# A graph layer and a mixture of experts in one kernel: the first round of messages joins the early part

## The reference

```
def _layernorm(x): return (x - mean) / sqrt(var + 1e-5)

# x 625 x 512; src, dst, edge_type: 10625 edges; 8 relations, two directions
H_all = einsum('rod,nd->rno', W_rel, ln(x)) + b_rel       # 16 products, 625 x 512 each
agg   = segment_sum(H_all[rel, dst], src) + segment_sum(H_all[rel + 8, src], dst)
x     = x + relu(ln(x) @ W_self.T + b_self + agg)

logits = ln(x) @ router_w.T                                # 16 experts, top 2, softmax of the two
x = x + sum over the two experts of share * ((silu(ln(x) @ gate) * (ln(x) @ up)) @ down)
```

## Time and profile before

| what | value |
|---|---|
| median of three runs | 791.1 us (788.78 to 797.87) |
| the profiled execution | 788.58 us, its span 786.7 us |
| TensorE busy | 722.4 us (92%), 3293 instructions |
| VectorE busy | 631.8 us (80%), 1273 instructions |
| ScalarE busy | 446.9 us (57%), 626 instructions |
| GpSimd busy | 259.8 us (33%), 263 instructions |
| mean granted TensorE clock | 0.957 of full speed |
| HBM | 176.46 MB read, 27.80 MB written |

### The profile page before, as it was taken

How to read it: one execution, slowest core, us unless ns; L and a number is a source line. 1 busy time by engine, 2 the same in 40 slices (tenths; PEclk the granted TensorE clock), 3 DMA queues, 4 the chain that set the end, 5 groups by cost and what they waited for, 6 DMA issues and landing times. The chain is left out here.

```text
span 786.7 us, 11209 instructions
## 1 busy us (share of the span) xinstructions
PE 722.4 (92%) x3293; PEld 568.4 (72%) x3293; DVE 631.8 (80%) x1273; ACT 446.9 (57%) x626; POOL 259.8 (33%) x263
## 2 busy tenths in 40 slices
PE   3699999999999999999788578999999999999994
PEld 3467777777677777878456557888888888888883
DVE  6769859888698866666679689989999899999890
ACT  2222235554355556555543446778888888887771
POOL 2000027661477577777772000111111111111101
PEclk9599999999999999999789597999999999999998
DMA  6534458884688788888862479988989999999932
GB/s 190 180 88 149 133 152 267 265 264 158 221 288 273 260 248 280 294 289 275 272 188 81 171 272 406 365 291 300 349 291 357 376 380 364 378 380 375 385 129 27
DMA packets 52077, 204.77 MB, mean 260 GB/s; under 512 B 9422, under 2 KB 9422, under 8 KB 37444
## 3 DMA queue, kind: packets, MB, share of 16 engines
q1 hardware_dynamic: 33108, 145.69, 50.1%
q0 software_dynamic: 18928, 58.60, 25.9%
HBM read 176.46 MB, written 27.80 MB: 260 GB/s over the span
## 5 line engine op out<-in xcount | busy, mean ns | idle before, releaser
L544 POOL DMA_INDIRECT rows_sb<-h_dram,row_of x190 | 211.4, 1113 | 200.5 <-DMA h_dram<-h_sb 134.7
L671 ACT COPY h_sb<-p_h 125x512 f32<-125x512 f32 x80 | 46.9, 586 | 179.6 <-PE p_h L725 179.6
L613 DVE TENSOR_TENSOR rows_lo<-rows_sb,rows_hi 128x512 fp32r<-128x512 f32 x190 | 130.2, 685 | 14.9 <-ACT rows_hi L677 14.8
L723 PE MATMUL p_h<-wt_hi_sb,xt_hi 128*125 128x512 f32 x320 | 127.0, 397 | 0.6 <-DVE wt_lo_sb L565 0.6
L724 PE MATMUL p_h<-wt_lo_sb,xt_hi 128*125 128x512 f32 x320 | 126.9, 397 | 0.0
L725 PE MATMUL p_h<-wt_hi_sb,xt_lo 128*125 128x512 f32 x320 | 126.7, 396 | 0.0
L677 ACT CAST rows_hi<-rows_sb 128x512 fp32r<-128x512 f32 x190 | 106.5, 620 | 15.3 <-DMA rows_sb<-h_dram,row_of 15.0
L565 DVE TENSOR_TENSOR wt_lo_sb<-w_nat,wt_hi_sb 128x512 fp32r<-128x512 f32 x64 | 44.0, 692 | 68.6 <-ACT wt_hi_sb L665 68.5
L742 PE MATMUL p_sum<-rows_hi,seg_hot 128*125 128x512 f32 x190 | 82.1, 432 | 8.2 <-DVE rows_lo L613 7.0
L972 POOL DMA_INDIRECT tokens<-token_dram,rows_of_tokens x16 | 15.7, 981 | 211.0 <-ACT rows_of_tokens L1183 164.3
L1005 DVE TENSOR_TENSOR g_lo_sb<-stage_gate,g_hi_sb 128x2048 fp32r<-128x2048 f32 x34 | 76.4, 2285 | 1.4 <-DVE later_tiles L1112 0.7
(11 more groups left out here) (236 smaller groups left out, 1376.4 us busy)
## 6 DMA issues: line engine op xcount, KB each, us to landing
stage_up<-in_L_ffn_up_w SPq DMA_DIRECT2D x32, 1024.0 KB, 6.6
stage_gate<-in_L_ffn_gate_w SPq DMA_DIRECT2D x30, 1024.0 KB, 7.7
stage_down<-in_L_ffn_down_w SPq DMA_DIRECT2D x30, 1024.0 KB, 7.0
h_dram<-h_sb SPq DMA_DIRECT2D x80, 224.0 KB
w_nat<-in_L_gnn_W_rel SPq DMA_DIRECT2D x17, 1024.0 KB, 8.0
rows_sb<-h_dram,row_of POOLq DMA_INDIRECT x190, 4.7
h_dram<-h_sb SPq DMA_DIRECT2D x80, 26.0 KB
stage_gate<-in_L_ffn_down_w SPq DMA_DIRECT2D x2, 1024.0 KB, 7.4
```

The source lines that it names most:

```text
L544: nc.gpsimd.indirect_dma_start(rows_sb[:, b % ROWS], None, h_dram[0:1 + made(n) * TP], bass.IndirectOffsetOnAxis(ap=row_of[:, b:b + 1].bit ...
L613: v.tensor_tensor(rows_lo[:, b % PARTS], rows_sb[:, b % ROWS], rows_hi[:, b % PARTS].bitcast(F32), ALU.subtract).then_inc(part_lo, 1)
L671: s.copy(h_sb[:, i % OUTS], p_h[0:TP, i % 2]).then_inc(h_taken, 1)
L723: m.matmul(o, xt_hi[:, dc, at], wt_hi_sb[:, j % 2, dc], start=False, stop=False)
```

## The change

The early part and the first round of messages become one block. The functions on_sync, on_gpsimd, on_vector, on_scalar and on_tensor hold both and take a flag `later`; a loop `nc.Fori(1, rounds)` with `later` set follows behind a barrier, for rounds 2 and up, and runs no time with these inputs. What was a buffer of one piece is now allocated for both. The sums of all rounds stay in `p_sum`, so `carry` and `first` and their loads go; b_self becomes a seventeenth row of the biases and comes in with one more matmul per tile. `x2` is the buffer of x. The list work of VectorE is grouped: `list_columns` writes the five columns of a chunk. LISTS, START and PACE have other values.

```
-LISTS = ((1, 5.5), (18, 2.5))
-LAG, START, PACE = 3, 17, 3.0
-LOW, BIASES = 32, 2 * R
+LISTS = ((5, 6), (26, 3))
+LAG, START, PACE = 3, 26, 3.1
+LOW, BIASES = 32, 2 * R + 1

 # SyncE
 for row in (0, LOW):
-    sp.dma_start(bias_f[row:row + BIASES], b_rel).then_inc(bias_loaded, 16)
-w_load(sp, 0, first_w_loaded)
-for t in range(T):
-    sp.dma_start(carry[:, t], b_self ... .to_broadcast([TP, D])).then_inc(carry_loaded, 16)
+    sp.dma_start(bias_f[row:row + 2 * R], b_rel).then_inc(bias_loaded, 16)
+    sp.dma_start(bias_f[row + 2 * R:row + BIASES], b_self ...).then_inc(bias_loaded, 16)
+w_load(0)
+w_load(1)
...
 for j in range(2 * R):
     if j:
         sp.wait_ge(w_low, KC * j)
-    w_load(sp, j + 1, w_loaded[(j + 1) % 2])
+        w_load(j + 1)
+    if j == 2:
+        for i in range(2):
+            sp.dma_start(stage_gate[:, 2 * i:2 * i + 2], gate_w[0][i]).then_inc(loaded["g"][i], 16)
     for t in range(T):
         store(T * j + t)
-sp.wait_ge(w_low, KC * WEIGHTS)
-w_load(sp, 0, next_w_loaded)
-sp.wait_ge(next_w_loaded, 16)

 # VectorE
+buckets()
+dve.wait_ge(bias_hi, 1)
+v.tensor_tensor(bias_parts[LOW:LOW + BIASES], ...).then_inc(bias_ready, 1)
 dve.wait_ge(x_loaded, 32)
 normal(0)
 normal(1)
...
 for t in range(2, T):
     normal(t)
     scales(t)
     low_columns(t - 2)
+    if t == 2:
+        for dc in range(KC):
+            w_rest(0, dc)
...
+v.tensor_copy(crow[:], p_counts)
 ranks(0)
 low_columns(T - 2)
 low_columns(T - 1)
 blocks_and_told()
 ranks(1)
 ranks(2)
...
+for dc in range(KC):
+    w_rest(1, dc)
 places()
 for i in range(PRODUCTS):
     j, t = i // T, i % T
-    if t:
+    if j and t:
         w_rest(j + 1, t - 1)
     for d in range(2):
-        for c in range(columns(d, i), columns(d, i + 1)):
-            column(d, c)
+        for n in chunks(d, i):
+            list_columns(d, n)
         if columns(d, i - 1) < EC and columns(d, i) == EC:
             read_list(d)
+            if d == 0:
+                round_count()
     for b in range(due(i), due(i + 1)):
         message(b)

+def list_columns(d, n):
+    nth, wide = (EC // HOT) * d + n, IN_DIR[d]
+    if nth >= HOT_SETS:
+        dve.wait_ge(list_taken, nth - HOT_SETS + 1)
+    for k in range(HOT):
+        c = n * HOT + k
+        v.tensor_scalar(lane_hot[:, nth % HOT_SETS, k], slot_iota[:], lane[:, d, c:c + 1], None, ALU.is_equal)
...
+    i.then_inc(list_hot, 1)

-then(v.tensor_tensor(carry[:, t], p_sum[0:TP, t], carry[:, t], ALU.add))
-then(v.scalar_tensor_tensor(x2[:, t], carry[:, t], 0.0, x_sb[:, t], ALU.max, ALU.add))
+then(v.scalar_tensor_tensor(x2[:, t], p_sum[0:TP, t], 0.0, x_sb[:, t], ALU.max, ALU.add))

 # ScalarE: s.copy(bias_parts[:], bias_f[:]) now stands first
     if t >= 2:
         turned_high(t - 2)
+    if t == 2:
+        for dc in range(KC):
+            w_main(0, dc)
 scaled(T - 1)
 turned_high(T - 2)
 turned_high(T - 1)
+for dc in range(KC):
+    w_main(1, dc)
 for i in range(PRODUCTS):
     take(i)
...

 # TensorE
 turn_x(0)
 ranks(0)
+turn_x(1)
+turn_x(2)
+pe.wait_ge(bias_ready, 1)
 for i in range(PRODUCTS):
     product(i)                  # for j == 0 it also waits for xt_ready
+    if i < 2:
+        turn_x(3 + i)
+    if 1 <= i < 3:
+        ranks(i)
     for d in range(2):
         for n in chunks(d, i - 1):
             list_chunk(d, n)
     for b in range(due(i - 1), due(i)):
         message(b)
...
 def self_product(t):
+    bias(p_sum[0:TP, t], 2 * R, False)
```

More of the change, by code:

```diff
@@ L182, in build @@
             n_rounds = sb("n_rounds", [1, 1], I32, g)
[L184 to L237, removed]
-                        sp.dma_start(bias_f[row:row + BIASES], b_rel).then_inc(bias_loaded, 16)
-                    w_load(sp, 0, first_w_loaded)
-                    for t in range(T):
[L241 to L247, removed]
-                    for i in range(2):
-                        sp.dma_start(stage_gate[:, 2 * i:2 * i + 2], gate_w[0][i]).then_inc(loaded["g"][i], 16)
-                    sp.wait_ge(spare_cleared, 48)
-                    sp.wait_ge(small_loaded, 16)
-                    sp.wait_ge(carry_loaded, 16 * T)
-                    sp.wait_ge(first_w_loaded, 16)
-                @block.gpsimd
-                def _(pool):
-                    q = nc.gpsimd
@@ new lines, in due, with columns, chunks, token_columns @@
+            def due(i):
+                return taken[max(i, 0)]
+            def columns(d, i):
+                begin, each = LISTS[d]
+                return max(0, min(EC, int(each * (i - begin))))
+            def chunks(d, i):
+                return range(columns(d, i) // HOT, columns(d, i + 1) // HOT)
+            def token_columns(a, t):
+                return a[:, :, t * TP:(t + 1) * TP]
+            def turned(t):
+                return p_sum[:, 3 + t % 2, 0:KC * TP].rearrange("p (c n) -> p c n", c=KC)
@@ new lines, in on_scalar @@
+                    for i in range(PRODUCTS):
+                        j, t = i // T, i % T
+                        take(i)
+                        if j and t:
+                            if t == 1:
+                                act.wait_ge(w_low, KC * j)
+                            w_main(j + 1, t - 1)
+                        for b in range(due(i), due(i + 1)):
+                            message(b)
+                    for b in range(due(PRODUCTS), last_span):
+                        message(b)
@@ new lines, in on_tensor @@
+                    for b in range(due(PRODUCTS - 1), last_span):
+                        message(b)
+                    pe.wait_ge(small_loaded, 16)
+                for t in range(T):
+                    if not later:
+                        self_product(t)
+                    for k in range(last_in_tile):
+                        message(last_span + t * last_in_tile + k)
+                    if t:
+                        turn(t - 1)
+                    if t > 1:
+                        token_logits(t - 2)
```

812 lines of the change are left out of this document (426 added, 386 removed).

## The result

The changed kernel takes 1231.3 us, median of four runs (1229.2 to 1234.4), where the kernel before took 791.8 us on the same chip: a ratio of 1.554, 95% interval 1.544 to 1.564. The forecast was 805, the range 786 to 817. It was wrong by more than 400 us, and the sign alone was right. Ratios here leave out executions that lie more than 1.5% above the fastest of their kernel, medians in us do not, and the traces of the kernel with the condition, of the one with the hint and of the one with a lag of four are of such slower executions.

What follows compares the result with a forecast made beforehand. The prediction took VectorE's gated wait for ScalarE's high weight part, with list columns and messages behind it, to bound the kernel. Terms -12.0 + 5.2 + 25.3 - 2.4 - 0.7 + 1.5 = +16.9, taken as +15, gave 805 us, range 786 to 817.

Steps and rivals of the forecast that it cites:

- a jump across the unused loop body: Behind the message stage: the loop body for later rounds is jumped over, 0.6 us, between 0 and 4.
- -12.0 + 5.2: Start of the products: product 0 starts 12.0 us sooner (8 to 14); turns and ranks moved among products cost 5.2.
- Product 0's copy: Sign at the start of the products: the copy of product 0 would stand near 28 us.
- the moved work: Turns and ranks among first products cost 5.2 us, 1.2 of it stall; take(0) stands behind turned_high(4) and weight splits.
- The lists: Beside the products: writing list columns in chunks of five costs 25.3 us, rounded 25, bounds 5 and 32.
- Direction 0: First list, steps 5 to 19, no messages: TensorE waits for grouped chunks, cost 9.7 us.
- Direction 1: Second list, beside messages, steps 27 to 54, 17 chunks: grouped chunks come late, cost 15.6 us.
- The pattern: Sign where messages and list run together: copies of products 6.6 us apart behind a chunk.
- where messages begin and resume: Direction 1, steps 26, 42 and 43: about 5 us more lost, within the list term.
- rival 3: Chunk steps: TensorE's clock falls, four to six falls at 2.5 us a product, 815 to 820 us; chance 0.12.
- 2.4 and 0.7: End of the message stage: gains of 2.4 us without the carry and 0.7 without the reload of weight 0.
- Rivals 1 and 2: List stalls: 1, lists stay covered, 783 us, chance 0.18; 2, they grow by some 14, about 795 us, 0.12.

Runs made afterwards that it cites:

- the kernel with the condition: Changed kernel, its loop for later rounds entered only where the count of rounds is above 1; ratio 1.027 to the kernel before.
- the one with the hint: Changed kernel with single columns, earlier weight loads, direction 1's lists two steps sooner, later rounds under a compare with branch hint; 798.6 us, ratio 0.982.
- the one with a lag of four: The kernel with the hint, messages due four steps behind their product, not three, and 3.2 a step instead of 3.1; ratio 0.999.
- the one pair: Changed kernel without the later round, columns grouped in chunks of five against written one by one; ratios 1.024 and 0.994 to the kernel before.
- product 79 in the other: Pair of the kernel before with its loop from 1 and the kernel before with columns grouped in chunks; ratios 0.998 and 1.026.
- loop from 1: Kernel before, its loop over rounds counting from 1 instead of 0 to the same limit; ratio 0.998.
- grouped: Kernel before with one edit, the lists' columns written in whole chunks of five; ratio 1.026.
- rows apart: Changed kernel with its empty round, whose gathers read 128 rows that lie apart instead of row 0 128 times; 1217.3 us, ratio 1.493.
- again: Changed kernel unaltered, run once more on chip 1; 1252.3 us, ratio 1.544 to the kernel before.
- no round: Changed kernel with the loop for later rounds and its barrier taken out; 833.9 us, ratio 1.024 to the kernel before.

## Why the prediction was wrong

**The step that failed** is one clause of the end: "a jump across the unused loop body, which no row prices: 0.6, between 0 and 4". There was no jump. The body ran, 421.7 us: a loop from 1 to 1 makes one pass. I took the loop for one that tests first, and the trace of before could not correct me: one pass with a count of 1 is what either kind of loop shows. That the loop makes a pass all the same should have been a rival; no chance was kept for it. Its price stood in the rows: the drain holds 19 gathers in 25.0 us, 1.32 us each, so 250 us for 190, and 170 columns at 0.48 and 0.60 us are 92 more: some 340 us. And when the jump is made, it costs about 4.1 us, just above my upper bound of 4. The Trainium skill, Advanced Engine Details and Errata, Control Flow Timing, gives 0.05 to 0.11 us for a branch. This jump over a long body does not agree: 4.1 us.

**Without that step** the sum was +15 to +17, of which 1.5 were for barrier, load and jump. The kernel without the loop has none of these three and a ratio of 1.024, +19 us on 789 (13 to 24 by the interval); the one with the condition has all and 1.027, +22. So the rest of the sum was somewhat low, and part of its agreement is luck, as the terms show:

*The early part.* Timelines of the changed kernel's start:

```profile
13.18 0.68 DVE L522 TENSOR_TENSOR bias_parts<-bias_f,bias_parts 17x512 fp32r<-17x512 f32 x1 [2.14 <-ACT bias_parts L618]
```
```profile
25.36 0.63 PE L696 MATMUL p_h<-wt_hi_sb,xt_hi 128*125 128x512 f32 x1
...
29.34 0.59 PE L665 MATMUL p_sum<-ident,xn_whole 125*128 125x125 f32 x4
...
36.60 0.50 PE L683 MATMUL p_h<-bias_parts,select 128*125 128x512 f32 x1 [1.29 <-ACT h_sb L597]
```

Product 0's first real matmul starts at 25.36 against 35.57: 10.2 us sooner, not 12.0. The bias waited 2.14 us for its high part, and that for the load of b_self until 12.53, so the first statistics start at 13.89, 3.3 us later than the earlier trace rows, where I had 1.3. The moved turn took 0.35 us at the high clock (29.34 to 29.69; I had 0.5), and product 2 stands 1.29 us for ScalarE's copy, where I had 1.2. At the copy of product 2 the lead is 6.3 us; -12.0 + 5.2 had said 6.8. That is close partly by luck: the gain is 1.8 us smaller, and the cost up to there is 3.9. Product 0's copy, which I had wanted near 28 us, starts at 35.97, since it stands behind turned_high(4) and the weight splits on ScalarE; my own paragraph on the moved work said so, and the sign contradicted it.

*The lists.* Direction 0: 62.1 us against 50.1 before, from product 5 to 19 by the table, +12.0, forecast +9.7. (My parts, six of 1.0 to 1.1, two of 1.9 and one of 2.0, add up to 11.8 to 12.4 and not to the 11.4 that I wrote.) Direction 1: 197.3 against 173.0, +24.3, forecast +15.6. The pattern came as worked out: 6.67 us between copies where a chunk stands behind a message step, 4.40 where none does:

```profile
203.11 0.58 ACT L597 COPY h_sb<-p_h 125x512 f32<-125x512 f32 x1 [1.75 <-PE p_h L698]
209.78 0.59 ACT L597 COPY h_sb<-p_h 125x512 f32<-125x512 f32 x1 [3.93 <-PE p_h L698]
214.18 0.58 ACT L597 COPY h_sb<-p_h 125x512 f32<-125x512 f32 x1 [1.74 <-PE p_h L698]
```

Isolated, the grouping costs 21.9 us in the one pair (6.7 and 15.2 in the two directions) and 25.1 at product 79 in the other; I had 25.3. What I missed in direction 1 is a transfer:

```profile
139.76 0.62 ACT L591 CAST wt_hi_sb<-w_nat 128x512 fp32r<-128x512 f32 x1 [4.34 <-DMA w_nat<-in_L_gnn_W_rel]
```

The first ten gathers now go out beside a weight's load, and the two copies behind it are 7.0 and 7.3 us apart. I had about 5 us for where messages begin and resume, from VectorE's work alone; the weight was in no term. Where messages resume, the copies of products 43 and 44 stand 9.55 us apart: TensorE waits 1.86 us for the chunk and then makes its product at the lower clock (granted 0.56 from 232.6 to 236.5). The +24.3 holds for the first chip. On chip 2 the same stretch takes 196.5 us without the round and 183.4 in the kernel before with its loop from 1, +13.1, since there the kernel before loses time itself: its copies 43 and 45 come 9.95 and 8.27 us behind the one before. From product 22 to 79 it is 283.1 us against 259.7, +23.4, where I had 275 and +16.

*The clock, rival 3.* It fell, at 58.5 to 62 us and three times more up to product 57 (near 97, 141 and 233 us): 0.95 and 0.97 over the two list stretches where before it was 1.00. Rival 3, with a chance of 0.12, thus came true in large part, beside the forecast. At half speed for a tenth of 62 us and 6% of 197 that is an estimate of 3 + 6 us, part of the two excesses above. On chip 2 the kernel before, with its loop from 1, has 0.97 over its direction 1 too. The stall before the fall at 58.5 was 2.05 us, for the chunk of product 8's step.

*The end.* From the copy of product 79 to the logits 59.8 us against 61.7: gain 1.9, where 2.4 and 0.7 stood. That pair does not settle it: on the other chips this part takes 63.3 and 65.4 us in variants of the kernel before (loop from 1, grouped), and 66.4 to 72.1 in the changed kernel (rows apart, again, no round). So the gain is not shown beyond the first chip; the spread is larger than the term.

The range of 786 to 817 would have held a kernel with the loop tested first: 1.027 x 791.8 = 813.5. Rivals 1 and 2 are out: the grouping alone costs over 20 us.

## What to carry to other kernels

Ask of every loop whether it may run zero times, and whether the construct allows it; if the trace of before can't tell, give the full body a price and a chance, however plain the source reads. A grouping that leaves the work of each engine as it is can still cost 3%, if it moves a batch's last element behind a gate; count the time at which the batch is ready, not its sum. When work moves earlier, look at which transfers now leave in the same step: the load issued one group sooner took away a stall of 6.6 us, and the whole early start was worth 9 at the same places.

## What the runs showed of the hardware

- A gather that reads one row of DRAM 128 times held a DMA engine 23.0 us in sum, against 15.2 for 128 different rows, and such gathers moved 155 GB/s at a DMA share of 0.9. An empty round is thus not cheap: its 190 messages took 312 us, 1.6 us each.
- A taken jump over a long loop body, on all engines, put about 4.1 us more between two parts, with and without a hint, and five packets of instructions came in that time; entering the loop without a jump, with the load of its count, cost some 0.6.
- The round ran TensorE at the 1.2 GHz level for over 400 us (granted clock 0.52 and 0.53 in its two parts). In the first it was busy for 40 of 109 us; in the second it had a wait in nearly every message, for a low part that VectorE makes of gathered rows.
- The first chip and chip 1 agree on the round to 0.03 us (421.68 and 421.65), though the kernel before takes 791.8 us on the one and 815.6 on the other.
